# A top-one expert layer in a decoder kernel: all experts on all tokens, against tokens sorted into tiles of one expert each

## The chip, the cores and the metric

The kernel runs on one core of a Trainium2 chip. The metric is the device time of one execution in microseconds (us), the median of several runs. The engines are TensorE (PE; its weight loads are shown as PEld), VectorE (DVE), ScalarE (ACT), GpSimd (POOL) and SyncE (SP), which here only issues transfers. Sixteen DMA engines move data between the device memory and SBUF, the memory on the chip. Matrix products land in PSUM, eight banks of 128 x 512 float32.

## The reference, cut to what matters

The program is a two-layer decoder over 1024 tokens of width 128. The change touches only the last part, the expert half of the second layer's feed-forward block. Everything is float32, with D = 128, eight experts and a hidden width of 256.

```python
h2 = rmsnorm(x, ln2_w)                       # x: 1024 tokens x 128
logits = h2 @ Wr + br                        # 1024 x 8
top1 = jnp.argmax(logits, axis=-1).reshape(-1)
u = jnp.einsum('td,edf->tef', xt, W1) + b1   # xt is h2; f = 512
u1, u2 = (u[..., :HID], u[..., HID:])        # HID = 256
act = u1 * jax.nn.sigmoid(u2)
y_all = jnp.einsum('teh,ehd->ted', act, W2) + b2
y = jnp.take_along_axis(y_all, top1[:, None, None], axis=1)[:, 0, :]
return x + y.reshape(batch, seq, DIM)
```

The reference works all eight experts for every token and then takes one. The result of this block is added to the residual and is the output.

## The kernel before

Six parts run one after the other, each in blocks of its own with a barrier between the blocks. The last part is `gqa_experts`. Its block `gqa_project` starts at 1304 us of the span, and there SP also fetches what the expert layer needs: among it all of W1 (`w1`, 2 MB), W2 (`w2`, 1 MB) and the biases. After attention and an output projection, the block `top_expert` starts at 1552.9 us and runs to the end.

In `top_expert` tokens lie as eight groups (NT = 8) of 128, one token to a partition. DVE works the scale of each token (`stats`, `mv`, `scale`) and the scaled rows `h`. PE turns the eight groups (L115, in `transpose_tiles`) and ACT copies them out of PSUM with the norm's weight on them as `hT`, 128 x 1024 (L3244). Then PE walks the experts in a fixed order of its own stream. For each expert e and each half q of the hidden width it makes the gate half and the value half for all 1024 tokens (L3304: four products of 128 x 512), and while the next expert's first layer runs it makes the second layer of the expert before (`expert_out`, L3291: 16 products of 128 x 128). ACT takes the sigmoid of the gate half (L3252), DVE multiplies it with the value half (L3203, `act_T`). `keep` (L3192) is the selection: DVE multiplies the expert's output by a column of `own`, which is 1 where the token belongs to this expert and 0 elsewhere, and POOL adds the kept part to the residual (L3235). `own` is made once (`choose`, L3174 to L3180) from the router's logits (`route`, L3263); the second biases go in by a product with `own` turned around (L3270, L3277). At the end DVE adds the last expert in two halves and SP stores them with two plain transfers (L3227).

A float32 product shows in the trace as two PE instructions, called passes below. A transpose is one pass. In the names, `gqa_experts_w` and `gqa_experts_b` stand for w1 or w2 and for b1 or b2, since numbers are left out of names.

Of the kernel before, what the change touches and what calls it, by code (L numbers as in the profile page):

```python
# [16 lines left out]
ALU = mybir.AluOpType  # L17
# [3 lines left out]
U8 = mybir.dt.uint8  # L21
AX = mybir.AxisListType.X
# [2624 lines left out]
N_PREFETCH = 11 + HQ  # L2647


def gqa_experts(nc, g, t, m):  # L2650
# [6 lines left out]
        ("ln_w", [P, 1]), ("w_r", [P, NE]), ("b_r", [P, NE]), ("order", [P, NE]),  # L2657
        ("w1", [P, NE, 2 * EH]), ("b1", [P, NE, 4]), ("w2", [P, NE, 2, D]), ("b2", [NE, D]))}
# [18 lines left out]
def gqa_project(nc, g, t, m, a):  # L2677
# [29 lines left out]
    with nc.Block() as block:  # L2707
        @block.sync
        def _(sp):
            for dst, src in ((w[:], t["L1_Wqkv"]), (bias[:], t["L1_bqkv"].to_broadcast([P, WQKV])),  # L2710
# [6 lines left out]
                sp.dma_start(dst, src).then_inc(loaded, 16)  # L2717
            wt = a["weights"]
            for dst, src in ((wt["b_g"][:], t["L1_bg_rep"].rearrange("o d -> d o")), (wt["w_o"][:], t["L1_ffn_Wo"]),
# [8 lines left out]
            sp.dma_start(wt["b1"][:], t["L1_eb1_T"].rearrange("(e q p) -> p e q", e=NE, p=P),  # L2728
                         allow_slow_non_contiguous=True).then_inc(a["prefetched"], 16)

            sp.wait_ge(a["zeroed"], 1)
# [382 lines left out]
def top_expert(nc, g, t, m, a):  # L3114


    ps = g["psum"]
    x1 = a["xn"]

    ln_w, w_r, b_r, w1, b1, w2, b2, order = (  # L3120
        a["weights"][n] for n in ("ln_w", "w_r", "b_r", "w1", "b1", "w2", "b2", "order"))
    stats, mv = m.sb("stats", [P, NT, 6]), m.sb("mv", [P, NT, 2])
    scale = m.sb("scale", [P, NT])
    h, hT = m.sb("h", [P, NT, D]), m.sb("hT", [P, S])
    best = m.sb("best", [P, NT])
    rank = m.sb("rank", [P, NT, NE])
    own = m.sb("own", [P, NT, NE])
    logits = m.sb("logits", [P, NT, NE])
    sig = m.sb("sig", [P, 2, S])
    act_T = m.sb("act_T", [P, 2, 2, S])  # L3130
    kept = m.sb("kept", [P, 2, NT, D])
    own_T = m.sb("own_T", [NE, S])
    oT_psum, oT_ready, bias_done, bias_read, result, stored = (
        m.sem(n) for n in ("oT_psum", "oT_ready", "bias_done", "bias_read", "result", "stored"))


    CHOOSE_AT, BIAS_AT = 0, 2

    chain_dve, scale_sq, scale_ready, h_ready, hT_psum, hT_ready, logit_done = (
        m.sem(n) for n in ("chain_dve", "scale_sq", "scale_ready", "h_ready",  # L3140
                           "hT_psum", "hT_ready", "logit_done"))
    u_done, sig_ready, act_ready, y_done, y_read, added, sum_ready = (
        m.sem(n) for n in ("u_done", "sig_ready", "act_ready", "y_done", "y_read", "added", "sum_ready"))

    def pair(n):
        return ps[:, 2 * n:2 * n + 2, :].rearrange("p b n -> p (b n)")

    with nc.Block() as block:
        @block.vector
        def _(dve):  # L3150
# [16 lines left out]
            link(dve.tensor_tensor(g["x"][:], g["x"][:], x1[:], ALU.add))  # L3167
# [4 lines left out]
            def choose():  # L3172
                dve.wait_ge(logit_done, 1)
                link(dve.tensor_tensor(logits[:], ps[:, 6, 0:NT * NE].rearrange("p (i e) -> p i e", e=NE),  # L3174
                                       b_r[:].unsqueeze(1).to_broadcast([P, NT, NE]), ALU.add))
                link(dve.reduce_max(best[:], logits[:], AX))
                link(dve.tensor_tensor(rank[:], logits[:], spread(best[:]), ALU.is_equal))
                link(dve.tensor_tensor(rank[:], rank[:], order[:].unsqueeze(1).to_broadcast([P, NT, NE]), ALU.mult))
                link(dve.reduce_max(best[:], rank[:], AX))
                dve.tensor_tensor(own[:], rank[:], spread(best[:]), ALU.is_equal).then_inc(sum_ready, 1)  # L3180
                dve.wait_ge(sum_ready, 1)
# [249 lines left out]
```

## Time and profile before

| what | us |
|---|---|
| median of 3 runs (1659.08 to 1662.02) | 1660.23 |
| the profiled execution, its own time | 1659.78 |
| its span, first to last instruction or landing | 1657.9 |
| block `top_expert` within it | 1552.9 to 1657.9 |
| PE busy over the span | 1369.8 (83%) |
| mean granted PE clock | 0.933 |

The profiled execution took 1.88 us more than its span, and 0.45 us less than the median. Steps that are worked out below are counted from the first instruction of `top_expert`, at 1552.92 us. "Idle before" in a row names what ended an engine's idle time. PEclk is the granted clock of TensorE: 1.00 is 2.4 GHz and 0.50 is 1.2 GHz.

### The profile page before, as it was taken

To read this page: it belongs to the slowest core of one execution; us is meant where nothing else is said; L and a number is where in the kernel's file an instruction comes from. 1 tells how busy PE (TensorE), PEld (TensorE's weight loads), DVE (VectorE), ACT (ScalarE), POOL (GpSimd) and SP (SyncE) were. 2 spreads that over 40 slices of the span, in tenths; PEclk is the share of its full clock that TensorE was granted. 3 is DMA by queue.
4 is the path that set the end of the run, shared out by engine and by line. 5 is a ranking of instruction groups with operands and counts; after the bars stand their busy time and mean duration, and the time that the engine had idled before them with its cause. 6 is when DMAs were issued, how large, how long until landed. Compare 5 with 4: busy or idle time off the path is not lost. (4 is left out here: it accounts for less than half of the span.)

```text
span 1657.9 us, 19830 instructions
## 1 busy us (share of the span) xinstructions
PE 1369.8 (83%) x6709; PEld 729.4 (44%) x6763; DVE 1255.7 (76%) x2833; ACT 897.2 (54%) x1424; POOL 678.3 (41%) x466
## 2 busy tenths in 40 slices
PE   6677699999997757889899988989875459999798
PEld 2223344333344434355555555555564323333465
DVE  5999567866515669999999999999878657776433
ACT  4666211457543320687778778877852146666311
POOL 2656111112101034688787878878861120000012
PEclk9799899999997878999999999999987759999899
DMA  6000011000005832000000000000040300000000
GB/s 152 1 0 1 28 58 49 0 1 0 1 0 125 174 103 63 1 1 1 1 1 1 1 1 1 1 1 1 7 152 1 89 1 1 1 1 1 1 0 14
DMA packets 32482, 42.99 MB, mean 26 GB/s; under 512 B 14286, under 2 KB 25644, under 8 KB 30992
## 3 DMA queue, kind: packets, MB, share of 16 engines
q1 hardware_dynamic: 29820, 29.61, 6.2%
q10 hardware_dynamic: 2552, 12.02, 3.5%
q8 instruction: 56, 0.92, 0.2%
q14 instruction: 54, 0.44, 0.1%
HBM read 33.48 MB, written 8.14 MB: 25 GB/s over the span
## 5 line engine op out<-in xcount | busy, mean ns | idle before, releaser
L1631 PE MATMUL psum<-film_ka,film_context_qa 97*128 97x427 bf16 (+3 forms) x896 | 329.8, 368 | 74.3 <-DVE film_stage_kept L1810 29.4
L2033 ACT ACTIVATE film_stage_e<-psum,film_stage_bias 128x512 f32<-128x512 f32 (+1 forms) x416 | 273.9, 668 | 96.9 <-PE psum L1633 87.0
L1810 DVE MAX8 film_stage_kept<-psum 128x8 f32<-128x213 f32 (+1 forms) x960 | 318.5, 377 | 6.6 <-PE psum L1633 6.3
L1633 PE MATMUL psum<-film_kb,film_context_qb 128*128 128x427 bf16 (+2 forms) x843 | 306.4, 364 | 0.0
L1882 POOL TENSOR_TENSOR film_stage_e<-film_stage_e 128x1024 f32<-128x1024 f32 (+1 forms) x91 | 207.1, 2276 | 80.7 <-DVE film_stage_e L1852 60.8
L1852 DVE SCALAR_TENSOR_TENSOR film_stage_e<-psum,film_context_top,film_stage_e 128x512 f32<-128x512 f32 (+1 forms) x325 | 231.8, 719 | 8.4 <-ACT film_stage_e L2033 6.7
L1631 PEld LDWEIGHTS psum<-film_ka,film_context_qa 97*128 97x128 bf16 x896 | 92.1, 103 | 195.3 <-DVE film_stage_kept L1810 86.8
L3235 POOL TENSOR_TENSOR residual<-residual,top_expert_kept 128x1024 f32<-128x1024 f32 x7 | 16.5, 2351 | 294.9 <-DVE top_expert_kept L3192 294.9
L1913 PEld LDWEIGHTS psum<-ctx_rows,film_stage_mean_T 128*128 128x128 f32 (+1 forms) x816 | 121.9, 192 | 30.0 <-issue 3.3
L2998 DVE TENSOR_REDUCE gqa_attend_low<-psum 128x1 f32<-128x128 f32 (+7 forms) x128 | 94.1, 755 | 43.1 <-PE psum L2917 40.7
L1913 PE MATMUL psum<-ctx_rows,film_stage_mean_T 128*128 128x96 f32 (+1 forms) x816 | 119.9, 269 | 1.8
L1872 POOL TENSOR_TENSOR film_stage_e<-film_stage_e,film_stage_keep 128x512 f32<-128x512 f32 (+1 forms) x91 | 102.1, 1122 | 32.7 <-ACT film_stage_keep L2009 32.4
L1885 POOL TENSOR_TENSOR film_stage_mean<-film_stage_e 128x512 f32<-128x512 f32 (+1 forms) x91 | 111.8, 1229 | 7.1
L3035 ACT ACTIVATE gqa_attend_prob<-psum 128x512 f32<-128x512 f32 x192 | 84.9, 486 | 51.4 <-PE psum L2930 50.6
L1018 PE MATMUL psum<-cross_attention_prob,ctx_rows 128*97 128x512 f32 (+1 forms) x204 | 99.7, 612 | 12.4 <-ACT cross_attention_prob L1078 12.4
L342 POOL TENSOR_TENSOR mamba_drive<-mamba_relu,mamba_b_all 128x1024 f32<-128x1024 f32 x32 | 77.2, 2414 | 64.7 <-ACT mamba_b_all L467 34.6
L1633 PEld LDWEIGHTS psum<-film_kb,film_context_qb 128*128 128x128 bf16 x896 | 89.7, 100 | 30.4 <-issue 3.6
L1078 ACT ACTIVATE cross_attention_prob<-psum 128x1024 f32<-128x1024 f32 (+1 forms) x51 | 51.0, 1018 | 87.0 <-PE psum L1033 87.0
L1033 PE MATMUL psum<-oss_attention_qc_shifted,ctx_T 97*128 97x512 f32 (+1 forms) x204 | 97.4, 600 | 0.8 <-ACT oss_attention_qc_shifted L1065 0.8
L957 DVE TENSOR_REDUCE cross_attention_tops<-psum 128x1 f32<-128x1024 f32 (+1 forms) x56 | 61.3, 1109 | 36.6 <-PE psum L1001 36.5
L1001 PE MATMUL psum<-ctx_T,cross_attention_qc 97*128 97x512 f32 (+1 forms) x208 | 87.3, 576 | 0.7 <-issue 0.7
L1897 PE MATMUL psum<-ident,film_stage_mean 128*128 128x128 f32 (+1 forms) x408 | 78.4, 273 | 6.1 <-ACT film_stage_mean_T L1985 5.0
(548 smaller groups left out, 2540.3 us busy)
## 6 DMA issues: line engine op xcount, KB each, us to landing
film_kb<-film_k_rows ACTq DMA_DIRECT2D x4, 1601.0 KB
film_ka<-film_k_rows ACTq DMA_DIRECT2D x3, 1601.0 KB
ctx_T<-in_ctx_T SPq DMA_DIRECT2D x1, 2401.5 KB
gqa_experts_w<-in_L_ffn_W SPq DMA_DIRECT2D x1, 2048.0 KB
film_stage_e<-in_dft_ahead SPq DMA_DIRECT2D x1, 1728.0 KB, 8.7
film_k_rows<-cross_attention_film_hi SPq DMA_DIRECT2D x6, 256.0 KB, 2.0
film_k_rows<-cross_attention_film_mid SPq DMA_DIRECT2D x6, 256.0 KB, 2.0
film_k_rows<-cross_attention_film_low SPq DMA_DIRECT2D x6, 256.0 KB, 2.0
```

Source lines behind the costliest of these rows:

```text
L1018: last = pe.matmul(ps[0:CA, 6 + n, :], ctx[0:rows, k, :], prob[0:rows, k % 3, n * HALF:(n + 1) * HALF], start=k == 0, stop=k == KT - 1)
L1033: last = pe.matmul(ps[0:rows, 2 * (k % 2) + n, :], ctx_T[:, k * P:k * P + rows], qc_shifted[:, n * HALF:(n + 1) * HALF], start=True, stop= ...
L1631: pe.matmul(out, a["qa"][0:ROWS, h, rows], a["ka"][0:ROWS, h, c + b:c + b + cols], start=True, stop=False)
L1633: last = pe.matmul(out, a["qb"][:, h, rows], a["kb"][:, h, c + b:c + b + cols], start=False, stop=True)
L1810: last = dve.max(kept[:, h % 2, PER_PIECE * u + s, :], bank[:, lo:hi])
L1852: dve.scalar_tensor_tensor(out=w, in0=weigh_bank(n, h), scalar=a["top"][:, NH * i + h, TOP - 1:TOP], in1=w, op0=ALU.is_ge, op1=ALU.mult).t ...
L1872: link(pool.tensor_tensor(w[h], w[h], keep[:, k % KEEPS, 0:width], ALU.mult))
L1882: link(pool.tensor_tensor(pairs[:, :, 0, :], pairs[:, :, 0, :], pairs[:, :, 1, :], ALU.add))
L1885: pool.tensor_tensor(out, w[0], w[2], ALU.add).then_inc(mean_ready, 1)
L1913: last = pe.matmul(ps[:, 7, 0:DC], mean_T[0:r, n % 2, b:b + P], ctx[0:r, (c + b) // P, 0:DC], start=c + b == 0, stop=c + b + r == S2)
L2033: act.activation(e[:, n % RING, sub, 0:PIECES[u][1]], ps[:, SEARCH_BANKS + q % WEIGH_BANKS, 0:PIECES[u][1]], ACT.Exp, bias=bias[:, i % 2, ...
L2998: dve.tensor_reduce(low[:, b, i:i + 1], pair(2 * (step % 2), (i + 1) * P), AX, ALU.max, negate=True).then_inc(max_read, 1)
```

## The change

The expert layer no longer works each expert on each token. The host packs each expert's W1, W2, b1 and b2 into one row block of 128 x 900 floats (`L1_expert_w`). The prefetch of W1, W2, b1 and b2 in `gqa_project` is gone; in its place SP loads a small table (`plan`), the token numbers (`ids`) and one block of blank rows, and writes these 15 times to a new scratch tensor in device memory, `slots` (15 tiles of 128 rows of 260 floats; 2 MB).

In `top_expert` the start is the same up to `own`, except that POOL, not DVE, adds the residual and the attention result (`rest`). PE then counts, for each token, how many tokens before it have the same expert, and how many each expert has in all, with nine products. DVE works out from this how many tiles of 128 rows each expert needs (never more than 15 in all), the row number `place_u` of each token, and the expert of each of the 15 tiles (`owner`). POOL scatters the tokens' rows (scaled input, residual, token number) to `slots` with eight indirect transfers; ACT waits for all eight and reads the 15 tiles back in three plain transfers. SP reads each tile's expert number into a register and fetches that expert's weights, 450 KB, once per tile. PE, ACT and DVE work each tile with its own expert alone, and POOL scatters each tile's result to the output with one indirect transfer, where rows that carry no token have a number beyond the bound and are dropped. All 15 tiles are worked, whether they hold tokens or not.

```diff
-                             (wt["w1"][:], t["L1_ffn_W1"].rearrange("e p n -> p e n")),
-                             (wt["w2"][:], t["L1_ffn_W2"].rearrange("e (q p) d -> p e q d", p=P)),
-                             (wt["b2"][:], t["L1_ffn_b2"])):
+                             (a["plan"][:], t["dispatch_plan"]), (a["ids"][:], t["token_ids"])):
...
+            sp.wait_ge(a["blank_loaded"], 16)
+            sp.dma_start(g["slots"].rearrange("(k p) c -> p k c", p=P),
+                         a["blank"][:].unsqueeze(1).to_broadcast([P, NTE, ROW])).then_inc(a["prefetched"], 16)
...
+            dve.wait_ge(counted, 1)
+            link(dve.tensor_tensor(more[:], number.unsqueeze(2).to_broadcast([P, NE, NT]),
...
+            dve.tensor_copy(place_u[:], place_f[:]).then_inc(place_ready, 1)
...
+            dve.tensor_copy(owner[:], owner_f[:]).then_inc(owner_ready, 1)
+            def finish(k):
+                dve.wait_ge(y_done, k + 1)
+                dve.tensor_tensor(result[:, k, :], second_out(k), slot_rows[:, k, D:2 * D],
+                                  ALU.add).then_inc(result_ready, 1)
+            for k in range(NTE):
                 for q in range(2):
+                    dve.wait_ge(value_done, k + 1)
+                    dve.wait_ge(sig_ready, 2 * k + q + 1)
+                    dve.scalar_tensor_tensor(out=act_T[:, k, q, :], in0=value_out(k, q), scalar=weights[:, k, B1_AT + q:B1_AT + q + 1],
+                                             in1=sig[:, k, q, :], op0=ALU.add, op1=ALU.mult).then_inc(act_ready, 1)
+                if k >= 1:
+                    finish(k - 1)
...
+            sp.wait_ge(owner_ready, 1)
+            for k in range(NTE):
+                expert = sp.value_load(owner[0:1, k:k + 1], min_val=0, max_val=NE - 1)
+                sp.dma_start(weights[:, k, :], t["L1_expert_w"][bass.ds(expert, 1)].rearrange("o p n -> p (o n)")
+                             ).then_inc(weights_read[k], 16)
...
+            pool.wait_ge(place_ready, 1)
+            for i in range(NT):
+                pool.indirect_dma_start(g["slots"], bass.IndirectOffsetOnAxis(ap=place_u[:, i:i + 1], axis=0),
+                                        rows[:, i, :], None).then_inc(scattered, 16)
+            for k in range(NTE):
+                pool.wait_ge(result_ready, k + 1)
+                pool.indirect_dma_start(
+                    t["out"], bass.IndirectOffsetOnAxis(ap=slot_rows[:, k, 2 * D:2 * D + 1].bitcast(U32), axis=0),
+                    result[:, k, :], None, bounds_check=S - 1, oob_is_err=False).then_inc(stored, 16)
...
+            act.wait_ge(scattered, 16 * NT)
+            for n, (lo, hi) in enumerate(GROUPS):
+                act.dma_start(slot_rows[:, lo:hi, :],
+                              g["slots"][lo * P:hi * P, :].rearrange("(k p) c -> p k c", p=P)
+                              ).then_inc(group_read[n], 16)
...
+            turn(0)
+            turn(1)
+            for k in range(NTE):
+                first_layer(k)
+                if k + 2 < NTE:
+                    turn(k + 2)
+                if k >= 1:
+                    second_layer(k - 1)
+            second_layer(NTE - 1)
```

PE, near the end of the program before: one expert's second layer, 16 products, and the first layer of the next, eight products of 128 x 512. (The names of the waits are those of the first holder of a recycled semaphore and say nothing here.)

```order
5783 L3291 MATMUL psum<-gqa_experts_w,top_expert_act_T 128x128 [waits mamba_xi_ready,mamba_z_ready]
5784 L3291 MATMUL psum<-gqa_experts_w,top_expert_act_T 128x128 x15
5785 L3304 MATMUL psum<-top_expert_hT,gqa_experts_w 128x512 [waits mamba_z_ready,mamba_xi_copied]
5786 L3304 MATMUL psum<-top_expert_hT,gqa_experts_w 128x512
5787 L3304 MATMUL psum<-top_expert_hT,gqa_experts_w 128x512 [waits mamba_xi_copied]
5788 L3304 MATMUL psum<-top_expert_hT,gqa_experts_w 128x512
5789 L3304 MATMUL psum<-top_expert_hT,gqa_experts_w 128x512 [waits mamba_z_ready,mamba_xi_copied]
```

PE at the same place after: one tile's first layer (L3350, four products), the turning of the tile two ahead (L3338), and the second layer of the tile before (L3357 the bias, L3361 two products).

```order
5786 L3350 MATMUL psum<-top_expert_slot_T,top_expert_weights 128x128 [waits mamba_bc_done,mamba_dt_copied,mamba_read_ready,mamba_conv_done]
5787 L3350 MATMUL psum<-top_expert_slot_T,top_expert_weights 128x128 x3
5788 L3338 MATMUL psum<-ident,top_expert_slot_rows 128x128 [waits mamba_conv_done]
5789 L3357 MATMUL psum<-top_expert_weights,ones 128x128 [waits mamba_split_ready]
5790 L3361 MATMUL psum<-top_expert_weights,top_expert_act_T 128x128 [waits mamba_dt_copied] x2
```

An expert's 24 products, eight of them 512 wide, gave way to a tile's eight instructions of 128 x 128, with four waits on the first of them (the turned tile, the weights, and ACT and DVE having read what is overwritten).

POOL, the last block, before: seven adds of the kept part.

```order
719 L3230 UNCONDITIONAL_BRANCH [waits barrier_Pool_Activation_PE_DVE_SP_gather]
720 L3235 TENSOR_TENSOR residual<-residual,top_expert_kept 128x1024 [waits mamba_xi_ready,mamba_ctx_loaded]
721 L3235 TENSOR_TENSOR residual<-residual,top_expert_kept 128x1024 [waits mamba_xi_ready,mamba_taps_ready] x6
722 L3148 UNCONDITIONAL_BRANCH [waits mamba_taps_ready]
```

POOL, the same block after:

```order
720 L3263 MEMSET top_expert_ones 128x128
721 L3264 MEMSET top_expert_own 128x8
722 L3265 MEMSET top_expert_rows 128x8x4
723 L3267 COPY top_expert_rows<-gqa_experts_ids 128x8 [waits mamba_h_ready]
724 L3268 TENSOR_TENSOR top_expert_rows<-residual,gqa_experts_xn 128x8x128
725 L3274 DMA expert_slots<-top_expert_rows,top_expert_place_u 1920x260 [waits mamba_ctx_loaded,mamba_tap_done,mamba_xn_ready,mamba_hT_psum]
726 L3274 DMA expert_slots<-top_expert_rows,top_expert_place_u 1920x260 x7
727 L3278 DMA out<-top_expert_result,top_expert_slot_rows 1024x128 [waits mamba_split_ready] x15
```

POOL now issues 23 indirect transfers: eight stand between the plan and the first tile, 15 follow the results, one to a tile. Outside `gqa_project`'s transfers and `top_expert`, the order of each engine is word for word the same.

## Rows read from the trace of the kernel before

**Rows 1.** Busy time by stretch: us, then busy us and (instructions) by engine.

```profile
core 0: us, PE busy (x) PEld busy (x) DVE busy (x) ACT busy (x) POOL busy (x), PEclk, DMA share, GB/s
1575.00:1647.00 72.00, 72.00 (x345) 46.71 (x344) 26.54 (x21) 14.48 (x13) 14.11 (x6) 1.00 0.00 0
```

**Rows 2.** The chain of work that ended last: start, us, what.

```profile
1552.92 1.66 DVE top_expert_stats L3154 x8
...
1565.78 1.69 PE psum L3263 x16
...
1601.79 3.57 PE psum L3291 x32
1605.37 6.87 PE psum L3304 x16
...
1654.43 0.69 DVE residual L3219
```

**Rows 3.** Timeline of `top_expert`, its start, in order of time: start, us, instruction.

```profile
1558.52 0.69 ACT L3244 ACTIVATE top_expert_hT<-psum,gqa_experts_ln_w 128x512 f32<-128x512 f32 x1 [0.17 <-PE psum L115]
1567.50 0.22 DVE L3174 TENSOR_TENSOR top_expert_logits<-psum,gqa_experts_b_r 128x64 f32<-128x64 f32 x1 [0.33 <-PE psum L3263]
1568.78 0.22 DVE L3180 TENSOR_TENSOR top_expert_own<-top_expert_rank,top_expert_best 128x64 f32<-128x64 f32 x1
```

**Rows 4.** Stretches with the granted clock, as Rows 1: in attention, and early in `top_expert`.

```profile
1356.00:1360.00 4.00, 3.72 (x19) 1.87 (x18) 1.61 (x4) 3.10 (x4) 0.00 (x0) 0.50 0.00 0
1368.00:1372.00 4.00, 3.75 (x31) 1.43 (x32) 2.46 (x9) 2.24 (x5) 0.00 (x0) 1.00 0.00 0
...
1552.00:1556.00 4.00, 0.00 (x0) 0.00 (x0) 2.70 (x19) 1.49 (x2) 0.00 (x0) 0.84 0.00 0
1562.00:1564.00 2.00, 2.00 (x4) 0.97 (x3) 0.00 (x0) 0.92 (x1) 0.00 (x0) 0.50 0.00 0
1565.00:1566.00 1.00, 1.00 (x7) 0.57 (x5) 0.11 (x1) 0.00 (x0) 0.00 (x0) 1.00 0.00 0
```

**Rows 5.** Transfers by line: KB each, median us from issue to landing.

```profile
film_k_rows<-cross_attention_film_hi SPq DMA_DIRECT2D x6, 256.0 KB, 2.0
out<-residual SPq DMA_DIRECT2D x2, 256.0 KB, 2.3
film_w_vf<-split_queries_w_vf SPq DMA_DIRECT2D x1, 192.0 KB, 2.5
```

**Rows 6.** SP's queue, in order of time: start, us in the queue.

```profile
1304.52 0.33 SPq L2717 DMA_DIRECT2D gqa_project_w<-in_L_Wqkv  x1
1304.90 0.43 SPq L2717 DMA_DIRECT2D gqa_project_bias<-in_L_bqkv  x1
```

**Rows 7.** Register loads from SBUF: duration min/median/max in ns.

```profile
L2376 SPq TENSOR_LOAD <-film_context_count x1: 478/478/478, 1222.3 to 1222.3; - x1
```

**Rows 8.** Stretches in which the DMA engines were full, as Rows 1.

```profile
1316.00:1320.00 4.00, 0.95 (x6) 0.66 (x5) 3.88 (x6) 0.00 (x0) 1.89 (x2) 0.90 1.00 376
```

**Rows 9.** POOL's groups by line: busy us, mean ns of one.

```profile
L3235 POOL TENSOR_TENSOR residual<-residual,top_expert_kept 128x1024 f32<-128x1024 f32 x7 | 16.5, 2351 | 294.9 <-DVE top_expert_kept L3192 294.9
L329 POOL MEMSET ctx_T<- 1x6404 f32 x1 | 5.4, 5429 | 0.3 <-POOLq L3419 0.3
```

**Rows 10.** ACT's and DVE's groups of 128 x 128 by line, as Rows 9.

```profile
L1168 DVE SCALAR_TENSOR_TENSOR residual<-psum,threshold_experts_kept,residual 128x128 f32<-128x128 f32 x32 | 11.2, 350 | 0.9
L3035 ACT ACTIVATE gqa_attend_prob<-psum 128x128 f32<-128x128 f32 x32 | 8.6, 268 | 0.0
```

More of the change, by code:

```diff
@@ L3125, in top_expert @@
+    h, rest = rows[:, :, 0:D], rows[:, :, D:2 * D]
+    hT = m.sb("hT", [P, S])
+    ones = m.sb("ones", [P, P])
     best = m.sb("best", [P, NT])
[L3126 to L3134, printed above, removed]
@@ L3212, in _ @@
[L3212 to L3220 removed]
+            dve.wait_ge(logit_done, 1)
@@ new lines, in _ @@
+            link(dve.reduce_sum(tiles[:], more[:], AX))
+            link(dve.tensor_tensor(upto_tiles[:], tiles[:].unsqueeze(1).to_broadcast([P, NE, NE]), upto, ALU.mult))
+            link(dve.reduce_sum(ends[:], upto_tiles[:], AX))
+            link(dve.tensor_tensor(starts[:], ends[:], tiles[:], ALU.subtract))
+            link(dve.scalar_tensor_tensor(out=place[:], in0=starts[:].unsqueeze(1).to_broadcast([P, NT, NE]),
+                                          scalar=float(P), in1=before, op0=ALU.mult, op1=ALU.add))
@@ L3230, in _ @@
+            sp.wait_ge(stored, 16 * NTE)
         @block.gpsimd
         def _(pool):
[L3232 to L3236 removed]
+            pool.memset(ones[:], 1.0).then_inc(consts_set, 1)
+            pool.memset(own[:, NT, :], 0.0).then_inc(consts_set, 1)
+            pool.memset(rows[:, :, 2 * D:ROW], 0.0).then_inc(consts_set, 1)
@@ L3315, in _ @@
-            expert_out(NE - 1)
+            pe.wait_ge(hT_ready, 2)
+            for i in range(NT):
+                last = pe.matmul(ps[:, 6, i * NE:(i + 1) * NE], hT[:, i * P:(i + 1) * P], w_r[:], start=True,
+                                 stop=True)
+            last.then_inc(logit_done, 1)
+            pe.wait_ge(consts_set, 2)
+            pe.wait_ge(own_ready, 1)
+            pe.matmul(ps[:, COUNT_BANK, 0:(NT + 1) * NE], plan["before"], own[:].rearrange("p i e -> p (i e)"),
+                      start=True, stop=False)
@@ new lines, in _, with turn @@
+            for i in range(NT):
+                last = pe.matmul(ps[:, COUNT_BANK, (i + 1) * NE:(NT + 1) * NE], ones[:],
+                                 own[:, i:i + 1, :].to_broadcast([P, NT - i, NE]), start=False, stop=i == NT - 1)
+            last.then_inc(counted, 1)
+            def turn(k):
+                for n, (lo, _) in enumerate(GROUPS):
+                    if k == lo:
+                        pe.wait_ge(group_read[n], 16)
+                if k >= 2:
+                    pe.wait_ge(turned, k - 1)
+                pe.transpose(ps[:, TURN_BANK + k % 2, 0:P], slot_rows[:, k, 0:D],
+                             g["ident"][:]).then_inc(turn_done, 1)
@@ new lines, in first_layer @@
+            def first_layer(k):
+                pe.wait_ge(turned, k + 1)
+                pe.wait_ge(weights_read[k], 16)
+                if k >= 2:
+                    pe.wait_ge(sig_ready, 2 * (k - 1))
+                    pe.wait_ge(act_ready, 2 * (k - 1))
+                for out, first, done in ((gate_out, 2, gate_done), (value_out, 0, value_done)):
+                    for q in range(2):
+                        unit = first + q
+                        last = pe.matmul(out(k, q), weights[:, k, W1_AT + unit * P:W1_AT + (unit + 1) * P], slot_T[:, k, :],
+                                         start=True, stop=True)
+                    last.then_inc(done, 1)
```

234 lines of the change are left out of this document (104 added, 130 removed).

## The prediction

> **What bounds the kernel now.** I read the chain of waits first, since the change replaces one block whole. From 1559 us to the end the chain is PE's and nothing else's: per expert 3.57 us of second layer and 6.87 us of first layer, back to back [rows 2]. The table by stretches confirms it: between 1575 and 1647 us PE is busy 72.00 of 72.00 us at full clock, while ACT has 14 us and DVE 27 [rows 1]. So this block is bound by the number of PE passes, and whatever takes passes away takes time away until something else is last. The block takes 105.0 us, from 1552.92 to the end of the span at 1657.9: up to 1655.1 it computes [rows 2], then the last store is issued and lands in 2.3 us [rows 5].
>
> **What the change removes.** Eight experts cost 8 x (3.57 + 6.87) = 83.5 us of PE [rows 2], and with them go the selection on DVE, the adds on POOL, and the products for the second bias. The prefetch of W1 and W2 ran beside other work with nothing waiting for it; the 2 MB of blank rows take its place in the same queue, 200 us before they are needed. I cost that at nothing. If that cover were gone, 2 MB at 376 GB/s [rows 8] would be 5.6 us.
>
> **What it adds, step by step**, in us after 1552.92. It is a chain through every engine, so I add it up.
>
> 1. The turned `hT` is complete at 1559.21 [rows 3], as before: 6.3.
> 2. Routing is 16 passes. They took 1.69 us at full clock [rows 2]. Before, eight wide products ran ahead of them and brought the clock up; now they come first, while the clock is at 0.50, where it still stood at 1564 [rows 4]. Twice 1.69 is 3.4: 9.7.
> 3. `own` is the same six DVE instructions, from 1567.50 to 1569.00 [rows 3], 1.5 us with a hop of 0.1 between engines: 11.3.
> 4. Counting is nine products, 18 passes; at the pace of step 2 at half clock 3.8: 15.1.
> 5. The token places are nine small DVE instructions, each waiting for the last. Such ones start 0.256 us apart (five steps from 1567.50 to 1568.78 [rows 3]): 2.3, with a hop 17.5. The owners are three more, ready at 18.3, and hold nobody but SP.
> 6. The scatter is eight indirect transfers from POOL. No indirect transfer and no transfer issued by POOL stands in the trace, and this is the dispute of the whole case. Call the time that POOL needs for one p. From below, SP puts a plain one in its queue in 0.33 us [rows 6]. From above, near: 2.35 us, POOL's instruction on 128 x 1024 [rows 9]. From above, far: POOL works alone, without the width of 128 partitions, at 5.43 us for 6404 elements [rows 9]; should an indirect transfer be work of that kind, p is up to 5.4. I take 1.3, the middle of the first two: it is a list of 128 numbers to be turned into 128 row addresses, more than SP's fixed copy, less than 131,000 elements. Eight are 10.4, and the last lands in 2.0 (256 KB to memory took 2.0 [rows 5]): 29.9.
> 7. ACT, queued behind all eight, reads the first two tiles, 266 KB: issue 0.4 and landing 2.5 [rows 5, 6], plus 0.5 since the weights are in the same DMA engines: 33.3.
> 8. Transpose of the first tile, copy by ACT (0.27 [rows 10]), hops: 34.0.
> 9. The tiles. One tile is 8 passes of first layer, 1 transpose, 2 for the bias, 4 of second layer, 15 in all. 32 passes of this size took 3.57 us [rows 2], so 0.112 each: 1.67 a tile, 25.1 for 15. The clock will be at 0.50 when they start, for PE has then been nearly idle for 18 us (it fell in the 4 us without PE work up to 1556, and was back between 1564 and 1565, some 8 us later [rows 4]); 8 us at half clock do the work of 4, so 4 more: 63.1. ACT's three instructions a tile are 0.8 us and DVE's three about 1.0 [rows 10], both below 1.67, and the order puts a whole tile of PE work between a gate and the second layer that needs it.
> 10. The last tile has no such cover: two sigmoids, two products, the last four passes and the add are about 1.3 from the end of its first layer; 0.7 of that is not in step 9: 63.8, and with the add 64.1.
> 11. The last store: p and 2.3 of landing [rows 5]: 67.7.
>
> Each tile's weights must be there in time. SP needs a register load, 0.48 [rows 7], and an issue, 0.43 [rows 6], with some register work: 1.1 a tile. The bytes, 461 KB at 376 GB/s [rows 8], need 1.23. So tile 14 has its weights at 18.3 + 18.4 + 2.5 = 39.2, where PE asks for them at about 61. The reading of the slots (2 MB) shares these engines, 5.6 us more at worst. Hidden, with 15 us to spare.
>
> The block becomes 67.7 instead of 105.0: 37.3 less. From the profiled execution's 1659.78 that is 1622.5, and by its distance to the median (0.45) **1623**.
>
> On p the Trainium skill, page "DMA: Bandwidth & Descriptors" (section "Latency and other measured facts"), gives a first byte after about 1 us for a transfer whose descriptors GpSimd writes. By it, as an estimate, p is 1.0, the nine p of this chain shrink by 0.3 each, and the sum would be 1620.
>
> **The rivals.**
>
> *POOL becomes the pace of the tiles.* Above p = 1.67 the stores fall behind PE. The chain is then 17.5 + 8p + 2.0 + 3.4 + 0.7 up to the first tile, 5.7 to its result at half clock, and 15p + 2.3: in all 31.6 + 23p. For p = 2.35 that is 85.7, or 1641. For it: POOL's ordinary instructions are slow. Against it: 128 numbers are little.
>
> *Slower than before, by the same queue.* 31.6 + 23p reaches 105 at p = 3.2. Beyond it the kernel is slower, and at the far bound of 5.4 it takes 156, or 1711. This needs POOL to go through the list one number at a time with a wait for each. The Trainium skill, page "GPSIMD Engine Reference" (section "Performance pitfalls for Q7 kernels"), has this mechanism for custom programs: 102 cycles for each read command, for example one for each index of a gather. At 1.2 GHz (page "Trainium Architecture — The Big Picture") that would be 10.9 us for 128, as an estimate, and 1837 by the same formula. No row here shows it.
>
> *The clock stays low.* All 225 passes at 0.50 are 50.2 instead of 29.1: 1644. For it: in attention PE was busy 3.72 us of 4 from 1356 and still stood at 0.50 [rows 4]. Against it: by 1368 it was at 1.00 with PE no busier, 3.75 of 4 [rows 4], and 15 passes against 0.8 us of ACT leave PE no gap.
>
> *The weights come late.* If a transfer whose source hangs on a register costs SP 3 us instead of 1.1, tile 14 is there at 66 and the block ends at 71.5: 1627. Within the range.
>
> *The change does not do what it says.* Even with all tokens on one expert 15 tiles are worked, so the data cannot undo the saving. If the read of the slots were late for tile 6, PE would stand for a few us, again within the range.
>
> **How the numbers follow.** Forecast 0.68 (late weights among it), POOL's pace 0.12, low clock 0.10, slower 0.07, other stalls that eat all of it 0.03. The low end: p = 0.33 takes 9 x 0.97 = 8.7 off, the clock coming back before routing and counting 3.6: 1611. The high end takes in POOL's pace at 2.35 and most of the low clock: 1643. About 0.2% is what a measurement of this kernel can tell from no change: faster by more 0.90, within 0.02, slower 0.08.
>
> **What would show it.** The profile after should have the first L3350 at 34 us into the block, the last at about 62, PE busy there without gaps, PEclk at 0.5 from routing to some 8 us into the tiles, L3274 in POOL's queue every 1.3 us, and the weights' transfers done by 40. If the L3278 follow each other without a pause while PE waits or is done, POOL is the pace. If PE's idle time is released by a landing of the weights, the loads are. The forecast is wrong above all if p is.

## The result and the profile after

| | before | after |
|---|---|---|
| median of 5 runs each, us | 1659.72 (1659.08 to 1662.02) | 1646.78 (1640.08 to 1651.64) |
| the profiled execution, us | 1659.78 | 1650.64 |
| its span, us | 1657.9 | 1648.5 |
| first instruction of `top_expert`, us | 1552.92 | 1556.66 |
| from there to the end of the span, us | 105.0 | 91.8 |
| mean granted clock | 0.933 | 0.910 |

The ratio of the times is 0.9922, 95% interval 0.9897 to 0.9947. The kernel is 13 us faster, where 37 were forecast; 1646.8 lies above the range's high end of 1643. The profiled execution is one of the slower ones of the changed kernel, so I compare its steps with the forecast's steps and return to the spread in an experiment.

The chain of waits of the kernel after (start, us, what) is the view that answers to [rows 2]. Its long part before the first tile:

```profile
1563.32 3.60 PE psum L3318 x16
...
1568.59 0.67 PE psum L3325 x2
1569.26 3.32 PE psum L3328 x16
...
1574.60 0.18 DVE top_expert_place_u L3229
...
1584.79 5.71 DMA expert_slots<-top_expert_rows,top_expert_place_u
...
1590.99 11.04 DMA top_expert_slot_rows<-expert_slots
```

Up to `place_u` it is what the forecast said, 18.1 us after the block's start. Then two transfers take 16.75 us between them: the last scatter, and the read of the second group of slots. The list of DMA issues (engine, count, KB each, median us from issue to landing) shows that the read is slow for all three groups, and which bulk shares the DMA engines with it:

```profile
top_expert_weights<-in_L_expert_w SPq DMA_DIRECT2D x15, 450.0 KB, 6.8
top_expert_slot_rows<-expert_slots ACTq DMA_DIRECT2D x1, 1170.0 KB, 13.8
top_expert_slot_rows<-expert_slots ACTq DMA_DIRECT2D x1, 520.0 KB, 11.0
top_expert_slot_rows<-expert_slots ACTq DMA_DIRECT2D x1, 260.0 KB, 7.7
```

Before, 256 KB landed in 2.0 us [rows 5]; now 260 KB take 7.7. The timeline says when the weights were issued and when PE got its first two tiles:

```profile
1576.46 16.76 SPq L3257 DMA_DIRECT2D top_expert_weights<-in_L_expert_w  x15
...
1598.26 0.69 PE L3338 MATMUL psum<-ident,top_expert_slot_rows 128*128 128x128 f32 x2 [25.69 <-DMA top_expert_slot_rows<-expert_slots]
1599.19 2.08 PE L3350 MATMUL psum<-top_expert_slot_T,top_expert_weights 128*128 128x128 f32 x8 [0.24 <-ACT top_expert_slot_T L3301]
1602.08 0.47 PE L3338 MATMUL psum<-ident,top_expert_slot_rows 128*128 128x128 f32 x1 [0.81 <-DMA top_expert_slot_rows<-expert_slots]
```

SP put all 15 tiles' weights, 6.9 MB, into its queue from 1576.5 to 1593.2, while the slots' read was issued only at 1590.5, behind 12 or 13 of them. PE stood 25.69 us before the first tile and, after a first layer, 0.81 more for the second group. The busy time by stretch (us, then busy us and (instructions) by engine, granted clock, DMA share, GB/s) is the view of [rows 1] and [rows 4]. The engines stand in the order PE, PEld, DVE, ACT, POOL:

```profile
1556.60:1585.00 28.40, 9.53 (x42) 8.87 (x42) 8.65 (x45) 4.35 (x6) 9.97 (x13) 0.55 0.26 86
1585.00:1602.00 17.00, 2.76 (x10) 2.07 (x10) 0.61 (x2) 1.25 (x4) 0.74 (x1) 0.50 1.04 400
1602.00:1627.00 25.00, 24.92 (x100) 21.42 (x100) 5.41 (x18) 6.96 (x21) 5.50 (x6) 0.50 0.11 37
1627.00:1643.00 16.00, 16.00 (x113) 13.57 (x111) 7.13 (x24) 6.24 (x20) 7.29 (x8) 0.98 0.06 23
```

The second line is the waiting: the DMA engines are full for 17 us, at 400 GB/s, and PE is busy 2.76. The third line is the second loss: for 25 us PE is busy without a gap, and its clock stays at 0.50, 1.2 GHz. Only the last line is the state that the forecast had for nearly the whole loop: 113 passes in 16 us against 100 in 25. One tile in each, from the chain:

```profile
1606.34 1.71 PE psum L3350 x8
1608.05 0.21 PE psum L3338
1608.26 0.72 PE psum L3357 x2
1608.99 1.15 PE psum L3361 x4
...
1630.63 0.89 PE psum L3350 x8
1631.52 0.11 PE psum L3338
1631.63 0.41 PE psum L3357 x2
1632.04 0.64 PE psum L3361 x4
```

The first of these two tiles takes 3.79 us and the second 2.06, where 1.67 was forecast for 15 passes at 0.112. The eight passes of the first layer (0.89) and the turning (0.11) keep that price. The two passes of the bias take 0.41 instead of 0.22 and the four of the second layer 0.64 instead of 0.45.

The way into the next experiments is then this account of the block, in us:

| part | forecast | profile after | difference |
|---|---|---|---|
| to `place_u` | 17.5 | 18.1 | 0.6 |
| scatter, to its last landing | 12.4 | 15.7 | 3.3 |
| from there to the loop's start on the chain | 4.1 | 11.6 | 7.5 |
| loop, to the last pass on the chain | 29.1 | 40.7 | 11.6 |
| last add, store and landing | 4.6 | 5.7 | 1.1 |
| sum | 67.7 | 91.8 | 24.1 |

The measured loop is not the whole of the forecast's. The two turnings and the first layer of the first tile were done before the second group landed, while PE would have waited for it, and the last tile's bias product and second layer run beside the store before it. So the 40.7 us hold 209 of the 225 passes; PE's own last pass ends at 1643.8.

### The profile page after: what moved, and what is told of

Read it like the earlier page. It is cut to its first block and busy times, and to the rows that moved or that the text cites. A ratio compares the mean times of both kernels' runs of the same rounds, so it can differ in the third digit from the quotient of the medians.

```text
span 1648.5 us, 19684 instructions
## 1 busy us (share of the span) xinstructions
PE 1335.4 (81%) x6544; PEld 718.3 (44%) x6598; DVE 1238.1 (75%) x2861; ACT 893.6 (54%) x1453; POOL 687.1 (42%) x487
## 5 line engine op out<-in xcount | busy, mean ns | idle before, releaser
L3011 DVE TENSOR_REDUCE gqa_attend_low<-psum 128x1 f32<-128x128 f32 (+7 forms) x128 | 94.1, 755 | 43.1 <-PE psum L2930 40.7
L1020 PE MATMUL psum<-cross_attention_prob,ctx_rows 128*97 128x512 f32 (+1 forms) x204 | 99.6, 611 | 12.4 <-ACT cross_attention_prob L1080 12.4
L655 POOL TENSOR_TENSOR ss_attention_s4d_i_decay<-cross_attention_s4d_ar,ross_attention_s4d_index 128x1024 f32<-128x1024 f32 x16 | 31.2, 1960 | 126.2 <-DVE ss_attention_s4d_i_angle L621 122.0
```

The lines of the kernel that those rows point to most:

```text
L1020: last = pe.matmul(ps[0:CA, 6 + n, :], ctx[0:rows, k, :], prob[0:rows, k % 3, n * HALF:(n + 1) * HALF], start=k == 0, stop=k == KT - 1)
L3011: dve.tensor_reduce(low[:, b, i:i + 1], pair(2 * (step % 2), (i + 1) * P), AX, ALU.max, negate=True).then_inc(max_read, 1)
```

## The experiments

Three theories stand against each other. A: the slots' read is late because the weights fill the DMA engines ahead of it. B: the clock, low for 25 us of tiles, costs the loop its time. C: something in the second layer costs more than its passes. I first took this to be the waits in PE's stream; the other candidate is the bias product, the one product of a tile whose operands have a single row. Every ratio is against the kernel before, run on the same chip in the same comparison.

**Weights later.** SP waits, before the sixth tile's weights, for the first group of slots to have landed. That leaves 2.3 MB of weights issued ahead of the read instead of nearly all.

```diff
             for k in range(NTE):
+                if k == 5:
+                    sp.wait_ge(group_read[0], 16)
                 expert = sp.value_load(owner[0:1, k:k + 1], min_val=0, max_val=NE - 1)
```

> The only edit: SP fetches the weights of the first five tiles at once and waits for the landing of the first group of slots (two tiles) before it fetches the other ten. Theory A (the reads of the slots stand behind 6.9 MB of weights in full DMA engines): the last scatter lands about 2.5 us after POOL is done with it instead of 4.8, the first group lands about 3 us after its issue instead of 11.0, the first tile starts some 10 us earlier, and the median is 8 to 11 us below that of the changed kernel, about 1637. Rival: the way through device memory is slow by itself (rows written one by one and read at once); then the landings stay at 4.8 and 11 us and nothing is gained.

Measured: 1629.70 us (1629.46 to 1630.14), ratio 0.9818 (0.9794 to 0.9842). From its chain of waits and its list of DMA issues:

```profile
1582.31 3.93 DMA expert_slots<-top_expert_rows,top_expert_place_u
...
1586.26 2.97 DMA top_expert_slot_rows<-expert_slots
...
top_expert_slot_rows<-expert_slots ACTq DMA_DIRECT2D x1, 520.0 KB, 4.3
top_expert_slot_rows<-expert_slots ACTq DMA_DIRECT2D x1, 260.0 KB, 3.0
```

The first group lands in 3.0 us instead of 7.7, the second in 4.3 instead of 11.0, and the last scatter takes 3.93 instead of 5.71. During the read of the first group (1586.3 to 1589.3) the DMA share is 0.67 at 178 GB/s, where it was 1.03 at 415 GB/s from 1590.5 to 1594 in the kernel after. The five tiles' weights had been moved by then: from 1585 to 1586 the share is 0.09. That shows A. Its size has to be read at a point that both chains pass. The second tile's first layer begins at 1592.50, 38.3 us into the block (which starts at 1554.19 here), and at 1602.55, 45.9 us into it, in the kernel after. So 7.6 us come from the order in which transfers were queued, and nothing else was changed. (From the first turning here, 35.1, to the loop's start there, 45.4, would be 10.3, but by then PE had already done a first layer.) The clock is the second thing that this run tells, by its stretches:

```profile
1589.00:1592.00 3.00, 2.48 (x10) 2.08 (x11) 0.00 (x0) 1.16 (x4) 0.00 (x0) 0.50 1.06 348
...
1593.00:1600.00 7.00, 7.00 (x52) 6.13 (x51) 2.70 (x9) 3.13 (x11) 1.99 (x2) 0.96 1.03 397
```

It was back at 1593.55, 4.3 us after the first turning at 1589.28, where the kernel after needed 29.5 us (1598.26 to 1627.8). So the gain is larger than A alone. The block is 73.2 us long instead of 91.8; of these 18.6 us the other 11.0 are the loop behind the second tile's start, with the clock up. The median is 17 us below the changed kernel's. The two streams differ in one more thing. Here the first one-row product begins after the clock is back; in the kernel after it runs at half clock, 6 us behind the first turning:

```profile
1593.99 0.48 PE L3359 MATMUL psum<-top_expert_weights,ones 1*128 1x128 f32 x2
...
1604.40 0.79 PE L3357 MATMUL psum<-top_expert_weights,ones 1*128 1x128 f32 x2
```

**Clock, with wide products.** Thirty more products of 128 x 512, into a bank that is not yet in use, fill PE's wait. They add work and remove nothing.

```diff
+            for _ in range(30):
+                pe.matmul(ps[:, GATE_BANK, 0:512], hT[:, 0:P], hT[:, 0:512], start=True, stop=True)
             turn(0)
```

> The only edit: between counting and the first tile PE makes 30 extra products of 128 x 128 by 128 x 512 whose results nobody reads, in the time in which it waits for the slots. Theory B (the 25 us at half clock are an after-effect of PE's idle wait, and cost about 11 us): PEclk is 1.00 from a few us after the extra products begin and stays there through all tiles, a tile takes 2.06 us from the first on instead of 3.79, the loop about 31 us instead of 40.7, median about 1637. Rival: the first seven tiles are slow because of something else that is late (weights, ACT) and the clock only goes with it; then the tiles still take 3.8 us at first. A second rival: passes of 128 columns with weight loads between them do not hold the clock, and it falls again during the tiles.

Measured: 1636.33 us (1631.15 to 1636.99), ratio 0.9849 (0.9819 to 0.9878). Its stretches (its second group lands in 10.7 us, which is no better than in the kernel after):

```profile
1573.00:1598.00 25.00, 24.69 (x59) 10.73 (x57) 0.00 (x0) 0.39 (x2) 7.92 (x8) 1.00 0.93 349
1599.00:1629.00 30.00, 29.83 (x216) 25.46 (x216) 13.22 (x44) 13.11 (x43) 12.79 (x13) 1.00 0.15 49
```

With the clock at 1.00 throughout, the chain goes from the second group's landing at 1599.36 to its last pass, ending at 1628.30, in 28.9 us instead of 40.7, for the same 209 passes. That shows B and sizes it: the low clock costs the loop 11.8 us in after's profiled execution. Extra work on PE made the kernel 10 us faster by the medians. Per tile the price is still 2.06, so the surplus of the second layer has nothing to do with the clock.

**Clock, with narrow products.** The same idea with products of 128 x 128, the shape of the tiles' own, to see whether narrow passes bring the clock back at all.

```diff
+            for _ in range(66):
+                pe.matmul(ps[:, GATE_BANK, 0:128], hT[:, 0:P], hT[:, 0:128], start=True, stop=True)
             turn(0)
```

> As the kernel with extra wide products, but 66 products of 128 x 128 by 128 x 128, 132 passes, the size of a tile's own, about 29 us at half clock. Theory B in its simple form (any unbroken work brings the clock back in some 8 us): PEclk is 1.00 after 8 us of them, and the tiles start at 1.00 or fall back only for a while. The other form (passes of 128 columns, with a weight load each, bring the clock back late or not at all, while those of 512 columns did before in 8 us): PEclk stays at 0.50 through most of the 29 us. Nothing else should move; the first tile still starts some 45 us into the block.

Measured: 1641.76 us in one run. Three stretches:

```profile
1573.00:1589.00 16.00, 10.71 (x96) 10.52 (x95) 0.00 (x0) 0.00 (x0) 5.76 (x6) 0.95 0.99 381
...
1610.00:1614.00 4.00, 4.00 (x18) 3.34 (x16) 0.90 (x3) 1.09 (x4) 1.19 (x2) 0.50 0.04 16
1614.00:1618.00 4.00, 4.00 (x28) 3.34 (x27) 1.80 (x6) 1.29 (x4) 1.46 (x2) 0.91 0.05 18
```

The extra products began at 1567.24 and the clock was at 1.00 from about 1570.4, so it does come back during narrow passes, 3 us into them and 7 us after PE began to count (1563.41) and had no gap any more. They ended at 1583.7, PE then stood 9.45 us, and the clock was down again at 1587.5, before the tiles. PE's first turning is at 1593.15, and from 1596.72 its stream has no gap; the clock returned at about 1614.7, 18 us later. It came back after 7 us of unbroken work once and after 18 us the other time, which neither form of the theory on record foresaw. What differs is what stands in the stream: the tiles have waits, turnings, and one product of one row in each.

**The bias product off PE.** DVE adds the bias to the residual part of the tile's rows, beside PE's work; PE's second layer waits once for both halves.

```diff
+            def add_bias(k):
+                dve.tensor_tensor(slot_rows[:, k, D:2 * D], slot_rows[:, k, D:2 * D], weights[:, k, B2_AT:B2_AT + D],
+                                  ALU.add).then_inc(biased, 1)
...
-                pe.matmul(second_out(k), g["ones"][0:1, 0:P], weights[0:1, k, B2_AT:B2_AT + D],
-                          start=True, stop=False)
+                pe.wait_ge(act_ready, 2 * k + 2)
                 for q in range(2):
-                    pe.wait_ge(act_ready, 2 * k + q + 1)
```

> The edit takes the bias product (two passes) off PE: DVE adds the second bias to the residual rows of the tile instead, beside PE's work; and the second layer has one wait for both halves of act_T instead of one for each. Theory C (each wait in PE's stream costs a bubble beside its passes: 2.06 us a tile where 15 passes at 0.112 are 1.67): a tile takes 1.5 to 1.65 us at full clock and 2.9 to 3.1 at half, 0.4 to 0.5 and 0.8 less, and the median is 7 to 9 us lower, about 1639. Rival: the tile's pace is set by the round trip through ACT and DVE, and the passes hide in it; then PE gets idle time and the pace stays at 2.06.

Measured: 1630.39 us (1628.58 to 1632.70), ratio 0.9824 (0.9797 to 0.9850). A tile at half clock, from the chain:

```profile
1599.71 1.71 PE psum L3357 x8
1601.42 0.21 PE psum L3345
1601.63 0.85 PE psum L3366 x4
```

The median is 9 us below the 1639 expected. A tile takes 2.77 us for 13 passes where 15 took 3.79: two passes less saved 1.02 us at half clock, where two at the forecast's pace are 0.45. And the clock was back at about 1603.6, 8.0 us after the first turning (1595.59) and 4.4 after PE's last gap (1599.23), and one second layer had by then run at half clock. The landings were those of the kernel after (7.7 and 10.9 us), so A has no part in this gain. But two things were changed at once here, the product and a wait.

**The bias product with 128 rows.** The tiles have the same instructions, passes and waits as in the changed kernel; only the bias product's operands have 128 rows, each row of the left one holding 1/128 (the bias is the same in all rows of the weights' tile). POOL fills the left operand once, early in the block, and PE waits for that once ahead of the first turning.

```diff
+            pool.memset(share[:], 1.0 / P).then_inc(share_set, 1)
...
-                pe.matmul(second_out(k), g["ones"][0:1, 0:P], weights[0:1, k, B2_AT:B2_AT + D],
+                pe.matmul(second_out(k), share[:], weights[:, k, B2_AT:B2_AT + D],
                           start=True, stop=False)
```

> The edit changes the second-bias product alone: ones over 128 divided by 128 times the bias on all 128 partitions, instead of one row of ones times one row; same number of passes, same waits. Theory D (the stretch at half clock is long because part of the tile's stream is a product of one row, which is light work): tiles last as long as before, 3.8 us at half and 2.06 at full clock, but full clock comes within 4 to 10 us of the first tile, the times are close together, median about 1637. Rival (only the number of waits and passes matters, as in the kernel with the bias on DVE): full clock comes as late and as unevenly as in the changed kernel, median about 1645.

Measured: 1632.83 us (1630.08 to 1632.91), ratio 0.9826 (0.9804 to 0.9849). Its chain, at full clock:

```profile
1603.47 0.89 PE psum L3352 x8
1604.37 0.11 PE psum L3340
1604.47 0.22 PE psum L3359 x2
1604.70 0.45 PE psum L3363 x4
```

1.67 us a tile, the prediction's figure to the hundredth, where the theory on record for this run had 2.06. This decides C. It is not the number of passes and not the waits, which are the same, but the single row: 0.19 us more for the product itself and 0.19 for its neighbours, 0.38 to 0.39 a tile. My first reading, that the waits cost the time, fell with this run. The clock was back at about 1602.5, 4.9 us after the first turning (1597.53). But that is before the first bias product of this run, at 1602.64, so this profile does not show what the product does to the clock. Feeding PE 128 rows of which 127 are redundant is 13 us faster than feeding it one (against the 1646.17 of the changed kernel beside it); 15 times 0.39, 5.8 us, are the price of the product, and the rest goes with the early clock.

**The changed kernel again**, beside the run just told, for its spread.

> The changed kernel itself, for its spread beside its own variants on one chip. Theory (its tiles start at half clock and the time until full clock differs from execution to execution): times spread over 8 us or more, median 1642 to 1647, where the kernel before spreads over 3 to 5. Rival (the first spread came from the other chip): times within 2 us of each other.

Measured: 1646.17 us (1639.20 to 1650.50), ratio 0.9898 (0.9863 to 0.9933). In its profiled execution, at 1650.50, the clock once more came back late:

```profile
1603.00:1626.00 23.00, 23.00 (x93) 19.67 (x93) 5.41 (x18) 5.96 (x18) 4.93 (x5) 0.50 0.07 25
```

The spread of 11 us is larger than that of the kernel before beside it (6.5) and about the size of the clock's 11.8. No quick run was profiled, but each run's mean granted clock is on record: 0.910 at 1650.50, 0.912 at 1649.62, 0.917 at 1642.71, 0.918 at 1639.20. The first five runs give the same order, from 0.910 at 1651.64 to 0.917 at 1640.08. 0.008 of the span is what some 26 us more at 0.50 make of it, so the quick runs are very likely those in which the clock came back early.

**Weights later and bias off PE.** The edits of those two runs together, cut here to their core.

```diff
+                if k == 5:
+                    sp.wait_ge(group_read[0], 16)
...
-                pe.matmul(second_out(k), g["ones"][0:1, 0:P], weights[0:1, k, B2_AT:B2_AT + D],
-                          start=True, stop=False)
+                pe.wait_ge(act_ready, 2 * k + 2)
```

> Weights of tiles 5 to 14 after the first group of slots, and the second bias on DVE with one wait, together. Theories A and C touch different stretches, so the gains should add up as far as PE is the pace: first tile 35 us into the block, then 1.45 us a tile, which is now POOL's pace (its stores follow each other without a pause) and not PE's; the end comes some 6 us before that of the kernel with the later weights alone: 1621 to 1624. Rival: the gains were the same thing twice (both brought the clock back early), then 1628 to 1630.

Measured: 1621.69 us (1618.83 to 1624.32), ratio 0.9770 (0.9745 to 0.9794). The stretch of the tiles, and three of POOL's stores in the timeline, two in the middle and the last:

```profile
1591.00:1610.00 19.00, 19.00 (x172) 19.00 (x172) 13.11 (x52) 11.89 (x39) 11.56 (x12) 1.00 0.69 266
...
1603.48 0.98 POOL L3287 DMA_INDIRECT out<-top_expert_result,top_expert_slot_rows  x1 [0.46 <-issue]
...
1604.93 0.98 POOL L3287 DMA_INDIRECT out<-top_expert_result,top_expert_slot_rows  x1 [0.47 <-issue]
...
1613.36 0.98 POOL L3287 DMA_INDIRECT out<-top_expert_result,top_expert_slot_rows  x1 [0.30 <-issue]
```

The block takes 65.0 us, from 1551.72 to the end at 1616.7. The sum that I had expected came out, its reason did not: I had thought that POOL would now be the pace. Its stores follow one another every 1.45 us, but so do PE's tiles, and PE is busy 19.00 of 19 us; at the end, where two results were ready, POOL needed 0.30 + 0.98 = 1.28 us for one. PE still sets the pace, and POOL is the next bound 0.2 us below it. The profiled execution is the fastest of its four.

**All three**, the last kernel with 16 wide products ahead of the first tile:

```diff
+            for _ in range(16):
+                pe.matmul(ps[:, GATE_BANK, 0:512], hT[:, 0:P], hT[:, 0:512], start=True, stop=True)
             turn(0)
```

> As the kernel with later weights and the bias on DVE, and with 16 of the extra wide products while PE waits for the slots. If POOL's stores are the pace from the third tile on, the clock is worth nothing more than the first two tiles: 1 to 2 us below that kernel, 1619 to 1622. Rival (PE's clock still counts through the tiles): 4 us or more.

Measured: 1620.18 us (1618.98 to 1620.95), ratio 0.9757 (0.9736 to 0.9778). It is the fastest version here, 2.4% below the kernel before and 1.6% below the changed kernel, but its interval overlaps that of the run without the wide products. The stretches say why the third edit brings so little:

```profile
1571.00:1586.00 15.00, 12.10 (x29) 5.05 (x27) 0.00 (x0) 0.00 (x0) 7.81 (x8) 1.00 0.71 244
1588.00:1590.00 2.00, 2.00 (x11) 2.00 (x11) 0.54 (x3) 0.96 (x3) 0.00 (x0) 0.50 1.07 362
1591.00:1610.00 19.00, 18.92 (x169) 18.73 (x169) 13.12 (x52) 11.43 (x38) 11.41 (x12) 1.00 0.68 262
```

Sixteen products end 3.63 us before the slots arrive, and the clock falls at about 1587.8, just as the tiles begin; it is back at 1591.1. The block is again 65.0 us. So the 1.5 us of the medians meet the forecast but are within the noise, and not for its reason, for PE and not POOL sets the pace here too.

## Why the prediction was wrong

The direction held and so did the mechanism: eight experts on each token are gone, and what replaces them is a chain through every engine and then a stream of PE passes. The time fell outside the range because three terms were mis-sized: the landing of the slots' read (step 7), the price of the passes and the time at half clock (both step 9).

*Steps 1 to 5, right.* Routing took 3.60 us at half clock (3.4 forecast), the counting 0.67 + 3.32 = 3.99 (3.8), and `place_u` was ready after 18.1 us (17.5). The clock fell at 1559.5, and both steps ran at half of it, as said.

*Step 6, p right, the landing not.* The dispute of the whole case went as forecast. POOL's scatters in the timeline (start, us, instruction, idle before):

```profile
1577.19 0.97 POOL L3274 DMA_INDIRECT expert_slots<-top_expert_rows,top_expert_place_u  x1 [0.30 <-issue]
1578.47 0.96 POOL L3274 DMA_INDIRECT expert_slots<-top_expert_rows,top_expert_place_u  x1 [0.30 <-issue]
```

They follow each other every 1.26 to 1.28 us, against 1.3 forecast. The rival in which POOL sets the pace needed 1.67 and had no part. The Trainium skill gives about 1 us to the first byte of a transfer whose descriptors GpSimd writes (page "DMA: Bandwidth & Descriptors", section "Latency and other measured facts"). The trace does not show a first byte; it has POOL busy for 0.96 us with each, and 0.30 between two. The Trainium skill's 102 cycles for each read command, for example for each index of a gather (page "GPSIMD Engine Reference", section "Performance pitfalls for Q7 kernels"), are for custom programs. They would have been 10.9 us by my estimate, and no transfer here took POOL more than 1.19. But the first scatter began 0.9 us after `place_u`, and the last took 4.75 us to land after POOL was done with it, where I put 2.0: the weights were already in the DMA engines. With ten of the 15 held back it took 2.97 (3.93 from its start).

*Step 7, the first error.* "Plus 0.5 since the weights are in the same DMA engines" should have been 5.2 for the first group, 7.7 us against 2.5, and the second group, at 11.0 us, set the loop's start. I had asked only whether the weights come late for PE ("hidden, with 15 us to spare") and not what they do to others on their way. The numbers for it stood in my own text: 461 KB every 1.1 us is 419 GB/s, above the 376 of [rows 8] at which I had the DMA engines full, and SP starts 14 us before ACT's read. An estimate from the trace gives the delay: by 1590.5 SP had issued some 5.8 MB and the DMA engines had moved 4.7 MB, about 1.1 of them the scatter's. So some 2 MB were left, or 5 us at 400 GB/s. The run with the weights later shows the whole effect, scatter and both groups: 7.6 us. Of the paragraph on the weights the other half was right: SP took 16.76 us for 15, 1.12 each.

*Step 9, the second error, the price of a pass.* I took 0.112 us for all 15 passes from 32 products with 128 rows. It holds for 13 of them (1.45 us a tile without the bias product, 1.67 with a 128-row one). The two of one row, and the four of the second layer behind them, cost 0.39 more. At full clock 209 passes took 28.9 us in the run with wide products, against 23.3 at the forecast's price: 5.6. The forecast took no bound for it. The trace of before has no one-row product, but it has the nearest thing, the second biases as sixteen passes with eight rows, between wide products:

```profile
1571.87 3.44 PE psum L3304 x8
1575.31 1.98 PE psum L3277 x16
1577.28 3.63 PE psum L3304 x8
```

Sixteen passes at 0.112 are 1.79, so these are 0.19 over, and the wide products behind them are 0.19 over those ahead. The same two amounts stand in a tile of the kernel after, for two one-row passes and the passes behind them. That looks like a price for the change of shape, in and out, and not for each pass; no run separates the two.

*Step 9, the third error, the clock.* "8 us at half clock" were 25.7 of the loop (1602.08 to 1627.8). The rival "the clock stays low", 1644, had a tenth of the chances, and is what most of this execution's loop did: the low clock cost 11.8 us, against 4 forecast, 7.8 more. These 7.8 and the 5.6 of the passes are 13.4; the 16 passes that the measured loop does not hold (1.8 at the forecast's price) bring it to the table's 11.6. Counted from the first turning, the clock came back after 29.5, 29.5, 21.6 and 4.3 us in the four profiles that have the one-row product and began their tiles at half clock (the kernel after, the same again, narrow products, weights later). Without the one-row product it took 8.0 us with the bias on DVE, 4.9 with the 128-row product and 4.3 with weights later and the bias on DVE.

*Steps 10 and 11.* The tail, from the last pass on the chain, was 5.7 us against 4.6. The last two results were ready close together, at 1643.08 and 1644.14, and POOL needed 1.28 us between their stores.

*The other differences.* The block began 3.7 us later than in the trace of before. The change touches only transfers there, with nothing waiting for them; PE's granted clock between 1530 and 1552 us was 0.78 against 0.92 in before's. The eight profiles of the variants and of the changed kernel again began the block between 1551.5 and 1556.5, on both sides of before's 1552.9. So this is most likely run variation and no cost of the change. Together 24.1 in the block, 3.7 ahead of it and 0.3 more between span and time make the 28.1 us by which the profiled execution (1650.6) misses the forecast for it (1622.5).

*The chances.* "Faster" had 0.90 and was right. The rivals stood side by side with a time of their own each; that a late landing, a dearer pass and a longer time at half clock come together in one execution had almost no weight in the high end.

**Open.** Why the clock came back after 4 to 8 us from the first turning in some profiles and after 22 to 30 in others is not shown. The likely cause is the one-row product: in all three slow profiles it ran while the clock was still at 0.50 (from 1604.40 in the kernel after), and with weights later the clock was back before the first of them. But of the profiles without that product only the one with the bias on DVE made a second layer at half clock; in the others the clock was back before the first, so they say nothing of it. That one also has one wait less in a tile. It shares with the three slow ones a gap of PE ahead of the loop (0.64 us there, 0.56 to 0.97 in the three), so the gap does not by itself keep the clock down. The times speak for the one-row product too: the four runs of the bias on DVE lie within 4.1 us and the four of the 128-row product within 2.8, and their lowest mean clock is 0.914, where five of the changed kernel's nine runs have 0.910 to 0.912. In the run with wide products the clock was up when the one-row products began, and it stayed up.

## What to carry to other kernels

A bulk load that is "hidden" is not free for its neighbours: before queueing megabytes early, look which small transfer on the critical chain comes behind them, and hold the bulk back with one wait on that small transfer (two lines, 17 us by the medians, of which 7.6 are shown to be this). Price a product by a row of its own shape, rows of the operands included; a bias goes cheaper on an idle vector engine, or as a product with as many rows as its neighbours. After a long wait of TensorE sum the loop once at full and once at half clock, and let the range reach both.

## What was not expected of the hardware

- A product of one row is dearer than one of 128 rows: 0.41 us against 0.22 for its two passes at full clock, between products of 128 rows, and 0.64 against 0.45 for the four passes that follow into the same bank; at half clock the 13 passes without it take 2.77 us, the 15 with it 3.79.
- In a stream that keeps TensorE busy 24.92 of 25 us the clock can stay at 0.50. It did so in the three profiles in which one-row products ran at half clock; without them it was back 4 to 8 us after the first turning.
- An indirect transfer of 128 rows costs GpSimd 0.96 to 0.98 us, and 1.26 to 1.28 from one to the next, for rows of 1040 bytes into `slots` and of 512 bytes into the output alike.
- 260 KB queued on ACT, with some 2 MB (an estimate, above) of what SP had issued still to be moved, landed in 7.7 us instead of 3.0. The Trainium skill says of this (page "DMA: Bandwidth & Descriptors", section "Issuing engines are not separate DMA queues") that transfers of all issuing engines interleave on the same 16 DMA engines. The trace agrees: the DMA share is 1.04 while both are under way, at 400 GB/s, and another engine's queue gave the small read no way past.
